# A routed feed-forward kernel: token-list entries of 64 bytes instead of 4, and tiles of neighbouring entries

## What is computed

```python
x = x + xattn(layernorm(x), ctx, mask)             # x: (16, 112, 512), ctx: (16, 375, 512)
# feed-forward on h = layernorm(x), 1792 tokens
probs = softmax(h @ gate_weight.T)                 # 64 experts
top_val, top_idx = top_k(probs, 8); top_val /= sum(top_val)
# ranks 5 to 8 may be sent on to a similar expert; gate_up: 512 -> 2*192, down: 192 -> 512
out = x + sum over the 8 experts of top_val * down(silu(gate(h)) * up(h))
```

## Time and profile before

| | us |
|---|---|
| median of 3 runs | 867.94 |
| profiled execution | 862.66 |
| its span, first to last instruction | 860.9 |
| PE busy in the span | 693.2 (81%) |
| DVE, ACT, POOL busy | 528.5, 459.6, 516.5 |
| stage 1, until the last entry is issued | 237.9 |
| first matmul of an expert (L1232) | 267.2 |

### The profile page before, as it was taken

How to read it: one execution, slowest core, us unless ns; L and a number is a source line. 1 busy time by engine, 2 the same in 40 slices (tenths; PEclk the granted TensorE clock), 3 DMA queues, 4 the chain that set the end, 5 groups by cost and what they waited for, 6 DMA issues and landing times. The chain is left out here.

```text
span 860.9 us, 15404 instructions
## 1 busy us (share of the span) xinstructions
PE 693.2 (81%) x4264; PEld 566.3 (66%) x4264; DVE 528.5 (61%) x1291; ACT 459.6 (53%) x900; POOL 516.5 (60%) x515
## 2 busy tenths in 40 slices
PE   5986868676017999999999999988998899999740
PEld 2544545343016999988888888877887778778630
DVE  4755736464125677776677777676776776776620
ACT  3543434232004676667666666767666676666520
POOL 2053535646716588888786676667676666666440
PEclk9997978885557999999999999999999999999965
DMA  8999986972047899999999999999999999999767
GB/s 274 351 333 157 214 189 132 182 201 64 2 143 232 192 256 264 248 259 263 248 245 276 269 271 275 286 242 273 279 248 253 269 265 265 256 249 260 152 120 164
DMA packets 103382, 196.36 MB, mean 228 GB/s; under 512 B 27697, under 2 KB 27825, under 8 KB 102850
## 3 DMA queue, kind: packets, MB, share of 16 engines
q1 hardware_dynamic: 70098, 121.70, 50.0%
q0 software_dynamic: 33200, 73.68, 40.7%
HBM read 147.23 MB, written 51.77 MB: 231 GB/s over the span
## 5 line engine op out<-in xcount | busy, mean ns | idle before, releaser
L1232 PE MATMUL bank<-xh,w1h 128*128 128x256 f32 (+7 forms) x768 | 227.7, 296 | 12.7 <-issue 4.5
L1233 PE MATMUL bank<-xl,w1h 128*128 128x256 f32 (+7 forms) x768 | 219.7, 286 | 0.0
L1234 PE MATMUL bank<-xh,w1l 128*128 128x256 f32 (+7 forms) x768 | 219.7, 286 | 0.0
L611 POOL DMA_INDIRECT xg<-normed_tokens,list x145 | 156.0, 1076 | 64.6 <-issue 49.3
L593 POOL DMA_INDIRECT list_table<-token,slot x112 | 107.5, 960 | 123.7 <-DVE token L781 91.3
L1232 PEld LDWEIGHTS bank<-xh,w1h 128*128 128x128 f32 x768 | 146.3, 190 | 17.2 <-issue 16.0
L635 POOL DMA_INDIRECT out_rows<-ys,list x73 | 117.4, 1608 | 62.1 <-ACT ys L1055 45.9
L635 POOL DMA_INDIRECT second_sum<-ys,list x70 | 111.9, 1599 | 59.7 <-ACT ys L1055 37.2
L1233 PEld LDWEIGHTS bank<-xl,w1h 128*128 128x128 f32 x768 | 146.5, 191 | 0.0
L1234 PEld LDWEIGHTS bank<-xh,w1l 128*128 128x128 f32 x768 | 146.3, 190 | 0.0
L925 DVE TENSOR_TENSOR xl<-bank,xh 128x448 fp32r<-128x448 f32 (+3 forms) x145 | 84.2, 617 | 90.0 <-ACT xh L1063 65.9
(11 more groups left out here) (205 smaller groups left out, 1123.9 us busy)
## 6 DMA issues: line engine op xcount, KB each, us to landing
raw<-in_w SPq DMA_DIRECT2D x195, 256.0 KB
raw<-in_w2a SPq DMA_DIRECT2D x65, 256.0 KB
ctxT_s<-in_ctxT SPq DMA_DIRECT2D x16, 768.0 KB
ctx_s<-in_ctx SPq DMA_DIRECT2D x16, 768.0 KB
raw<-in_w2b SPq DMA_DIRECT2D x65, 128.0 KB
second_sum<-zeros SPq DMA_DIRECT2D x18, 256.0 KB
x_in<-in_x SPq DMA_DIRECT2D x16, 224.0 KB
out_rows<-x SPq DMA_DIRECT2D x16, 224.0 KB
```

The lines of the kernel that those rows point to most:

```text
L611: pool.indirect_dma_start(xg[u.on(XGS)][0:u.m, t, :], None, normed, bass.IndirectOffsetOnAxis(ap=lists[u.on(LISTS)][0:u.m, t:t + 1], axis= ...
L1232: pe.matmul(bank[m][:, 0:W], wh, mh, start=(c == 0), stop=False)
L1233: pe.matmul(bank[m][:, 0:W], wh, ml, start=False, stop=False)
L1234: mm = pe.matmul(bank[m][:, 0:W], wl, mh, start=False, stop=(c == DK - 1))
```

## The change

- An entry of the table is a line of 16 int32 (64 bytes), of which the first is the token number. Lists begin 2064 lines apart (before: 2240 entries of 4 bytes), so 132,096 bytes instead of 8,960.
- The indirect DMAs of `enter` write 64 bytes per entry instead of 4, from `token` tiles that are 16 times as wide; their count, 112, stays.
- Blanks: 1920 lines of each list instead of 2048 entries. `blank` is [128, 128, 16] instead of [64, 512]; its four quarters of 32 partitions hold pad numbers 0 to 511. A piece of 128 lines of all lists is two DMAs of 256 KB (32 lists each, 8192 bytes per list). The first 640 lines are written in slot 1 (5 pieces, 10 DMAs), the other 1280 in slots 2 to 7 (10 pieces, 20 DMAs) under a semaphore of their own, `far_filled`, for which POOL waits before batch 5's entries. Before, all blanks were 4 DMAs of 128 KB in slot 1.
- POOL's preparation has five more memsets (`blank`, 8 KB a partition, and four `token` tiles) and four iotas for `blank` instead of one. POOL's wait for `filled` moves into `enter` of batch 0.
- List loads read lines of 64 bytes, and row p of tile t is now entry t*m + p: a tile takes m neighbouring entries. Gathers and scatters take their indices from the first column of the lines.
- The second buffers of `w1h` and `w1l` move into the memory that stage 1's buffers leave, to make room.

```diff
-LIST_PARTS = (2048, 192)
+LIST_PARTS = (2048, 16)
-FILLED = 2048
+FILLED = 1920
+LINE = 16
+BLANKS = 128
+NEAR = 640
-    table = nc.dram_tensor("list_table", (PAD_LIST + PADS, 1), I32, kind="Internal").ap()
+    table = nc.dram_tensor("list_table", (PAD_LIST + BLANKS, LINE), I32, kind="Internal").ap()
...
-        blank = sb("blank", [E, PADS], I32)
+        blank = sb("blank", [P, BLANKS, LINE], I32)
...
+            def fill_lists(i, done):
+                quarter = P // (PADS // BLANKS)
+                source = blank[i % (PADS // BLANKS) * quarter:(i % (PADS // BLANKS) + 1) * quarter].rearrange("p n c -> p (n c)")
+                per_expert = table[0:PAD_LIST].rearrange("(e n) c -> e (n c)", e=E)
+                for e in range(0, E, quarter):
+                    sp.dma_start(per_expert[e:e + quarter, i * BLANKS * LINE:(i + 1) * BLANKS * LINE], source).then_inc(done, 16)
...
-                for i in range(0, FILLED, PADS):
-                    sp.dma_start(per_expert[:, i:i + PADS], blank[:]).then_inc(filled, 16)
+                for i in range(NEAR // BLANKS):
+                    fill_lists(i, filled)
...
+                if s.n in FAR_AT:
+                    far = (FILLED - NEAR) // BLANKS
+                    for i in range(far * FAR_AT.index(s.n) // len(FAR_AT), far * (FAR_AT.index(s.n) + 1) // len(FAR_AT)):
+                        fill_lists(NEAR // BLANKS + i, far_filled)
...
-                rows = table[bass.ds(at, u.rows), :].rearrange("(p t) c -> p (t c)", p=u.m)
-                sp.dma_start(lists[u.on(LISTS)][0:u.m, 0:u.nt], rows).then_inc(list_in[u.on(LISTS)], 16)
+                rows = table[bass.ds(at, u.rows), :].rearrange("(t p) c -> p t c", p=u.m)
+                sp.dma_start(lists[u.on(LISTS)][0:u.m, 0:u.nt, :], rows).then_inc(list_in[u.on(LISTS)], 16)
...
+                if b.n == 0:
+                    pool.wait_ge(filled, FILLS * 16)
+                if b.n == NEAR // T:
+                    pool.wait_ge(far_filled, (FILLED - NEAR) // BLANKS * 2 * 16)
                 split_wait(pool, c_slots, (b.n + 1) * SLOTS)
                 for k in range(ENTERS):
                     pool.indirect_dma_start(table, bass.IndirectOffsetOnAxis(ap=slot8[b.four][:, k:k + 1], axis=0),
-                                            token[b.four][:, k:k + 1], None).then_inc(tabled[b.four], 16)
+                                            token[b.four][:, k, :], None).then_inc(tabled[b.four], 16)
```

More of the change, by code:

```diff
@@ L208, in program @@
         slot8 = [sb(f"slot8_{i}", [P, ENTERS], I32) for i in range(4)]
-        token = [sb(f"token_{i}", [P, ENTERS], I32) for i in range(4)]
+        token = [sb(f"token_{i}", [P, ENTERS, LINE], I32) for i in range(4)]
         prim = sb("prim", [E, E]); pen = sb("pen", [E, E]); simd = sb("simd", [E, E])
@@ L227, in program @@
         raw2 = two("raw2_", [P, 2, D])
-        w1h = two("w1h", [P, DK, 2 * F], F32R)
-        w1l = two("w1l", [P, DK, 2 * F], F32R)
+        w1h = [sb("w1h0", [P, DK, 2 * F], F32R)]
+        w1l = [sb("w1l0", [P, DK, 2 * F], F32R)]
         w2h = two("w2h", [P, 2, D], F32R)
         w2l = two("w2l", [P, D], F32R)
-        lists = [sb(f"list{i}", [P, 3], I32) for i in range(LISTS)]
+        lists = [sb(f"list{i}", [P, 3, LINE], I32) for i in range(LISTS)]
         over_list = sb("over_list", [P, 1], I32)
@@ L270, in program @@
         xg = [sb(f"xg{i}", [P, 3, ROW]) for i in range(XGS)]
+        w1h.append(sb("w1h1", [P, DK, 2 * F], F32R))
+        w1l.append(sb("w1l1", [P, DK, 2 * F], F32R))
         xh = two("xh", [P, DK, WIDE], F32R)
@@ L409, in _ @@
             CLEAR_AT = [B - 1, B, B + 1]
-            FILL_AT = 1
+            FILL_AT, FAR_AT = 1, range(2, 8)
             def load_x(b):
@@ L545, in _ @@
             nc.gpsimd.memset(zeros[:], 0.0).then_inc(const_pool, 1)
-            nc.gpsimd.iota(blank[:], [[1, PADS]], base=TOK,
-                           channel_multiplier=0).then_inc(const_pool, 1)
+            nc.gpsimd.memset(blank[:], 0).then_inc(cleared, 1)
+            for i in range(4):
+                nc.gpsimd.memset(token[i][:], 0).then_inc(cleared, 1)
+            pool.wait_ge(cleared, 6)
+            quarter = P // (PADS // BLANKS)
+            for i in range(PADS // BLANKS):
+                nc.gpsimd.iota(blank[i * quarter:(i + 1) * quarter, :, 0], [[1, BLANKS]], base=TOK + i * BLANKS,
+                               channel_multiplier=0).then_inc(const_pool, 1)
+            pool.wait_ge(const_pool, 2 + PADS // BLANKS)
             nc.gpsimd.memset(tri[:], -1.0).then_inc(cleared, 1)
@@ L567, in _ @@
             for i in range(4):
-                nc.gpsimd.iota(token[i][:], [[1, ENTERS]], base=T * (i - 4) - T * ENTERS,
+                nc.gpsimd.iota(token[i][:, :, 0], [[1, ENTERS]], base=T * (i - 4) - T * ENTERS,
                                channel_multiplier=ENTERS).then_inc(cleared, 1)
-            pool.wait_ge(cleared, 10)
+            pool.wait_ge(cleared, 15)
             nc.gpsimd.affine_select(out=spread_to[:], in_=spread_to[:], compare_op=ALU.is_ge, fill=0.0,
@@ L611, in gather @@
                     pool.indirect_dma_start(xg[u.on(XGS)][0:u.m, t, :], None, normed,
-                                            bass.IndirectOffsetOnAxis(ap=lists[u.on(LISTS)][0:u.m, t:t + 1], axis=0)
+                                            bass.IndirectOffsetOnAxis(ap=lists[u.on(LISTS)][0:u.m, t, 0:1], axis=0)
                                             ).then_inc(gathered[u.on(XGS)][t], 16)
@@ L634, in scatter @@
                     split_wait(pool, ys_s, u.t0 + t + 1)
-                    pool.indirect_dma_start((out, second)[u.sums()], bass.IndirectOffsetOnAxis(ap=lists[u.on(LISTS)][0:u.m, t:t + 1], axis=0),
+                    pool.indirect_dma_start((out, second)[u.sums()], bass.IndirectOffsetOnAxis(ap=lists[u.on(LISTS)][0:u.m, t, 0:1], axis=0),
                                             ys[u.on(2)][0:u.m, t, :], None, compute_op=ALU.add).then_inc(scattered[u.sums()], 16)
@@ L649, in keep_list @@
                 split_wait(pool, scattered[u.sums()], u.landed_before())
-                nc.gpsimd.tensor_copy(over_list[:], lists[u.on(LISTS)][:, 0:1]).then_inc(kept, 1)
+                nc.gpsimd.tensor_copy(over_list[:], lists[u.on(LISTS)][:, 0, 0:1]).then_inc(kept, 1)
             def scatter_over(u):
@@ L780, in publish @@
                 yield from ch.link(v.tensor_scalar(slot8[b.four][:], bank[7][:, 0:ENTERS], -1.0, float(PAD_LIST), ALU.mult, ALU.add))
-                yield from ch.link(v.tensor_scalar(token[b.four][:], token[b.four][:], 4 * T, None, ALU.add), tell=True)
+                yield from ch.link(v.tensor_scalar(token[b.four][:, :, 0], token[b.four][:, :, 0], 4 * T, None, ALU.add), tell=True)
                 ch.done()
@@ L1271 @@
 DVE_CONSTS = 13 + len(CAP_STEPS)
-CONSTS = 20 + 3 * NSENT
-FILLS = 2 * PADS // P + FILLED // PADS + 1
+CONSTS = 19 + PADS // BLANKS + 3 * NSENT
+FILLS = 2 * PADS // P + NEAR // BLANKS * 2 + 1
 NOVERS = 2 * E + 3 * MAX_OVER
```

14 lines of the change are left out of this document (6 added, 8 removed).

## The result

The changed kernel takes 876.91 us (median of 4 runs, 876.68 to 884.14), the kernel before beside it 867.71 (4 runs, 865.61 to 870.99): ratio 1.0143, interval 1.0097 to 1.0189. It is slower by some 9 us, where 817 was forecast. The profiled run took 876.74, its span is 875.0.

A forecast was written before the change was run, and what follows sets the result against it. It took stage 1 to be held up by 4-byte entry writes, with POOL's entry DMAs as lower bound. Terms -38.3 (pace), -13.9 (restart) and +1 (stage 2) sum to -51.2 us: 867.94 becomes 817, range 806 to 867.

The forecast's parts named there:

- What bounds the kernel now: Stage 1: 4-byte entry writes hold up the pipeline, leaving 47 us of gaps in POOL; savings there reach the end.
- both signs: Stage 1: DMA rate falls to 157 GB/s at a share of 0.95, and PE's results are taken late.
- The entries: Stage 1 entry DMAs: 64-byte lines end partial, colliding writes; bounds all or none of the hold-up, taken all.
- A rule against it: Entry writes: below 512 bytes a transfer needs a read-modify-write, so 64 bytes are no better than 4.
- The first entry: Start of stage 1's entries: blanks move the first entry DMA from 49.0 to 54 us.
- Near blanks: Slot 1 of stage 1: 2.10 MB more blanks delay the first entry by 4 us, bounds 0 and 10.8.
- Far blanks: Six later slots of stage 1: 5.24 MB, nearly covered by PE, cost 1 us, bounds 0 and 4.2.
- The pace: Stage 1 entries: POOL sets 141.6 us, ending at 195.6; gain 42.3, less 4 for PE coming late, 38.3 us.
- The restart: From the entries' end to the first expert matmul: 29.3 us becomes 15.4, gain 13.9, bounds 9 and 20.
- Stage 2: Expert stage: larger list loads cost 1 us, bounds 0 and 4; neighbouring entries 0, bounds -3 and +3.
- The third one: Rival: not the entries but something on POOL's side with any series of indirect DMAs; 875 us, chance 0.07.
- The first rival, no relief: Stage 1 entries: 64-byte writes hold up the core too, blanks cost 4 + 14; 886 us, chance 0.18.

The follow-up runs named there:

- 825 comparison: A set of runs side by side in which the unchanged kernel before took 825 to 826 us; in four other comparisons it took 868 to 879.
- the version with spread blanks: Changed kernel with blanks written from 128 partitions of 4 KB in 5 DMAs, not 32 of 8 KB in 10: 809.7 us, ratio 0.9787 to the kernel before.
- the paced one: Changed kernel with a memset and a wait for it between the entry DMAs of a batch: 836.7 us, ratio 1.0117 to the kernel before.

## Why the prediction was wrong

**What bounds the kernel now.** Right that stage 1 has 47 us of gaps and that what is saved there reaches the end: without entries the kernel takes 781. Wrong that one cause stands behind both signs. There are two. The low rate at a full share belongs to the 4-byte writes. The late takings belong to the series of indirect DMAs. The row that told them apart was read and not followed: in 220 to 240 us the DMA share is 0.02 and DVE still took PE's result 13 us late (it did two short instructions in between and was idle 5.96 us just before). A write, partial or not, can hardly be what delays a signal when the DMA engines are idle.

**The entries.** This is the step that failed. It took all of the relief, since whole rows ran at 390 GB/s before the first entry. The rate did rise as forecast, to 310 and 321 GB/s at 80 to 120 us. The gaps stayed, 57.8 us for 49.0, since the series holds up the pipeline whatever it moves: 256-byte reads 53.2, 512-byte writes 57.8. Removing one of two hold-ups that lie over each other gave nothing back. The prediction gave all of the relief, 38.3 us, to the size of the write; of that nothing came.

**A rule against it.** The Trainium skill, "DMA: Bandwidth & Descriptors", section Specifications, puts 64 bytes on the same side of its limit of 512 as 4. The prediction's inference from it, that 64 bytes are then no better, doesn't hold: at a share near 1.0, beside 4-byte entries the engines move 181 to 189 GB/s, beside 64-byte entries 350 to 377. The time of that rival, slower, came by another cause.

**The first entry.** Mis-sized, inside its bounds. Near blanks: taken 4, measured 9.0 (57.9 without the far blanks against 48.9). The term was priced at 390 GB/s; I had written that 32 source partitions might double the time and took less than that. Far blanks: taken 1, measured 0.3 to 1.3 of the first entry (58.3 to 59.3 against 57.9), and nothing of the time. POOL's longer preparation is not on the path: POOL had waited 48.3 us when the first entry came.

**The pace.** 16 * 8.85 us was right as the bound: the entry DMA takes 0.96 us with 64 bytes as with 4, and where no signal was late the entries ran from 52.2 to 196.6, 144.4 us.

**The restart.** 29.3 to 15.4 was forecast. The changed kernel has 23.5, 27.8 and 30.9 in its three profiles, the kernel before 29.3, 24.2 and 31.1, so of the 13.9 us forecast here none is shown. The weights are issued ahead of the last entry's end by only 3 us (251.40 against 254.35), because the plan is held up like the rest. Without late signals it was 19.8 (216.4 - 196.6), so 4 us of the gain were too much in any case.

**Stage 2.** Lists and order at +1: measured between 0 and 4. Inside the bounds.

**The rivals.** The third one happened, at 877 where it said 875, and had 0.07. That its time fits so well is in part luck: it is right that only the blanks then cost, but it says that the entries' bytes are no cause at all, and in an 825 comparison 512-byte writes in place of the 4-byte ones took 20 us less. The argument against it was that stage 2 issues 289 indirect DMAs with PE always busy. There they come in groups of two to six, with copies and waits of POOL between them; in stage 1 they come 7 to 21 back to back, 1.26 us apart. POOL's timeline in stage 2 of the changed kernel:

```profile
416.17 2.00 POOL L659 DMA_INDIRECT second_sum<-ys,list  x1 [0.30 <-issue]
418.48 0.97 POOL L635 DMA_INDIRECT xg<-normed_tokens,list  x1 [0.30 <-issue]
...
421.06 0.92 POOL L635 DMA_INDIRECT xg<-normed_tokens,list  x1 [0.30 <-issue]
421.99 0.50 POOL L650 COPY wt<-xg 96x3 f32 x1
423.00 1.50 POOL L659 DMA_INDIRECT out_rows<-ys,list  x1 [0.51 <-ACT ys L1079]
```

In 290 to 820 us of the changed kernel, ACT has a single idle time that ends with "remote", of 1.1 us, and DVE and PE none. In stage 1, a pause of 0.22 + 0.28 us between the DMAs went with entries 22 us shorter in all. What was a count of DMAs had to be read as a pattern in time. The first rival, no relief, got the sign right and the mechanism wrong: the far blanks that it priced at 14 cost nothing.

**What stays open.** How a series of indirect DMAs on POOL delays the signals of other engines; why it does so in some comparisons and in others not, on the same chip; whether a bare semaphore instruction would be enough of a pause; and what the changed kernel takes in an 825 comparison. From 809.7 for the version with spread blanks and 6 us of the first entry I estimate 816, and from 836.7 for the paced one less 19 of pause 818, both below 825.9, but neither was run. Such a time beside the forecast 817 would be luck: the gain would be 8 to 10 us, not 51. Open is also whether the signals are held by POOL's issuing or by something that the DMAs in flight do, since every run had both or neither. A version that waits for the landing of earlier entry DMAs wasn't tried either.

## What to carry to other kernels

When two signs of a hold-up go with the same instructions, look for a window in which only one of them is there before giving both one cause; here one window with an idle DMA queue and a late signal was enough. A cheap test comes before the rewrite: replace the suspected writes by reads, or leave them out, and see which part of the loss goes. And where signals are late, long back-to-back series of indirect DMAs on GpSimd are worth breaking with a short instruction of its own and a wait for it, and blanks worth writing from all 128 partitions: both together made this kernel 2.4% faster than before where the change alone made it 1% slower. Where no signal is late, the pause costs 19 us, and the kernel with the change and the pause was 1.2% slower than before; the spread blanks without it were 2.1% faster.

## What the runs showed of the hardware

During series of 7 to 28 indirect DMAs on GpSimd, ACT and DVE were idle for up to 12 or 13 us before they took results of PE (the longest is 12.2 us in the kernel before, 12.1 in the changed one, 13.4 with reads of 256 bytes, 12.2 with writes of 512 bytes), and in the kernel before and the changed one most of the waits over 5 us ended 1.5 to 2.7 us behind the end of a series. With a pause of about 0.5 us after each DMA the longest was 5.9 us. It was there in four comparisons and in neither of the other two, with two chips in both kinds; between them the time of the kernel before differs by 42 to 54 us.

Beside indirect writes of 128 entries of 4 bytes the DMA engines moved 181 GB/s at a share of 1.07; with 64 bytes an entry it was 377 GB/s at 1.04. The entries' own packets took 2.2 and 3.1% of the engines' time.

While blanks were stored from 32 SBUF partitions in pieces of 8 KB, the engines moved 262 GB/s at a share of 1.00; with 128 partitions and pieces of 4 KB, and other loads among them, 418 GB/s at 1.03.

GpSimd was busy 0.96 us with an indirect DMA of 128 entries, of 4, 64, 256 or 512 bytes each alike.
